# A decoder layer on one core: residual tiles queued behind the second pair of output weights, and two copies of ScalarE at another place

## The reference, cut to what matters

```python
x = _layernorm(x + _L0_attn_ref(x, wq, wk, wv, wo))        # 32 query heads, 8 key/value heads, window of 128
x = _layernorm(x + _L0_xattn_ref(x, ctx, s1, z1, s2, z2))  # matmul of two fake-quantised tensors
x = _layernorm(x + _L0_ffn_ref(x, w_gate, w_up, w_down))   # silu(gate) * up, truncated to int8, down
```

## Time and profile before

| | us |
|---|---|
| median of three runs (1465.59 to 1466.85) | 1465.61 |
| the profiled execution | 1466.88 |
| its span, first to last instruction | 1465.1 |
| TensorE busy | 1429.0 (98%) |
| VectorE busy | 999.4 (68%) |
| ScalarE busy | 782.7 (53%) |
| GpSimd busy | 740.7 (51%) |
| mean granted TensorE clock | 0.996 |

### The profile page before, as it was taken

The page is one execution under the profiler, slowest core; times in us unless marked ns, Lnnn a source line. Parts: engine busy times, 40 slices in busy tenths (PEclk is TensorE's granted clock), DMA queues, the critical chain, the costliest instruction groups (busy, mean ns, idle before and its releaser), DMA issues.

```text
span 1465.1 us, 22782 instructions
## 1 busy us (share of the span) xinstructions
PE 1429.0 (98%) x7024; PEld 1153.3 (79%) x7024; DVE 999.4 (68%) x1768; ACT 782.7 (53%) x1553; POOL 740.7 (51%) x651
## 2 busy tenths in 40 slices
PE   8899999999999999999999999999989999999997
PEld 6688888888888888888888888887657888778643
DVE  7644444445656578888888888887786656566597
ACT  5433333333345466666575666565466555555674
POOL 0477777777565454555455555554476333433100
PEclk9999999999999999999999999999999999999998
DMA  6477877776663757675757676763151222222611
GB/s 230 146 271 283 286 281 270 273 275 256 212 239 108 282 180 277 200 267 179 265 196 271 206 265 209 269 236 127 41 181 74 94 100 81 76 93 86 230 43 74
DMA packets 114330, 283.20 MB, mean 193 GB/s; under 512 B 21216, under 2 KB 21600, under 8 KB 114272
## 3 DMA queue, kind: packets, MB, share of 16 engines
q1 hardware_dynamic: 114272, 282.50, 55.1%
HBM read 184.94 MB, written 95.42 MB: 191 GB/s over the span
## 4 chain that ended last, share of the span: by engine, by line
PE 50%; DVE 7%; ACT 4%; DMA 3%; issue 3%; POOL 2%; SPq 0%; DVEq 0%; ACTq 0%; POOLq 0%
PE ps L1141 7%; PE ps L1143 7%; PE ps L1142 7%; PE ps L1297 6%; PE ps L1298 5%; PE ps L1350 5%; PE ps L1070 2%; PE ps L1071 2%; PE ps L1072 2%; PE ps L1118 2%; PE ps L1117 1%; PE ps L1119 1%; PE ps L1083 1%; DVE u_val L2853 1%; PE ps L1222 1%
## 5 line engine op out<-in xcount | busy, mean ns | idle before, releaser
L1051 PE MATMUL ps<-xo_h,wb_h 128*128 128x512 f32 x644 | 251.6, 391 | 5.2 <-DVE xo_l L2391 2.0
L1053 PE MATMUL ps<-xo_h,wb_l 128*128 128x512 f32 x644 | 250.7, 389 | 0.0
L1052 PE MATMUL ps<-xo_l,wb_h 128*128 128x512 f32 x644 | 250.6, 389 | 0.0
L1141 PE MATMUL ps<-wo_h,o_h 128*128 128x512 f32 x512 | 207.9, 406 | 1.7 <-DMA wo_l<-wo_low 1.7
L1143 PE MATMUL ps<-wo_h,o_l 128*128 128x512 f32 x512 | 200.3, 391 | 0.0
L1142 PE MATMUL ps<-wo_l,o_h 128*128 128x512 f32 x512 | 200.1, 391 | 0.0
L2166 POOL TENSOR_TENSOR pm_l<-pt_l,upto 128x512 fp32r<-128x512 f32 x58 | 74.8, 1290 | 230.4 <-DVE pt_l L2490 230.4
L1517 ACT ACTIVATE wb_h<-wf_l 128x512 fp32r<-128x512 f32 x69 | 43.6, 632 | 197.7 <-DVE wf_l L2419 82.2
L1051 PEld LDWEIGHTS ps<-xo_h,wb_h 128*128 128x128 f32 x644 | 120.9, 188 | 33.2 <-issue 5.8
L1566 ACT ACTIVATE prob<-prob,exp_bias 128x128 f32<-128x128 f32 x256 | 99.8, 391 | 85.6 <-DVE exp_bias L2477 85.6
L2131 POOL TENSOR_TENSOR wb_l<-wf_l,wb_h 128x512 fp32r<-128x512 f32 x66 | 87.8, 1330 | 112.7 <-DVE s_sum L2414 56.8
(11 more groups left out here) (259 smaller groups left out, 3557.8 us busy)
## 6 DMA issues: line engine op xcount, KB each, us to landing
raw<-w_att SPq DMA_DIRECT2D x47, 512.0 KB, 5.4
f_raw<-w_gu SPq DMA_DIRECT2D x44, 512.0 KB, 5.0
u_gu<-f_unit SPq DMA_DIRECT2D x42, 512.0 KB, 4.9
gq<-u_gu SPq DMA_DIRECT2D x42, 512.0 KB, 3.9
wp_raw<-w_att SPq DMA_DIRECT2D x32, 512.0 KB, 5.8
wo_high<-wp_h SPq DMA_DIRECT2D x32, 512.0 KB, 2.8
wo_low<-wp_l SPq DMA_DIRECT2D x32, 512.0 KB, 4.1
q_rows<-c SPq DMA_DIRECT2D x64, 256.0 KB, 2.7
```

Of the source, the lines that this page charges most:

```text
L1051: pe.matmul(prod_ps[i], wh, chunk(xo_h[i], c), start=(i in OPENS and c == 0), stop=False, skip_group_check=True)
L1052: pe.matmul(prod_ps[i], wh, chunk(xo_l[i], c), start=False, stop=False, skip_group_check=True)
L1053: last = pe.matmul(prod_ps[i], wl, chunk(xo_h[i], c), start=False, stop=(c == KH - 1), skip_group_check=True)
L1141: pe.matmul(into, oh, wo_h[half][:, h, :], start=(h == 0), stop=False)
```

## The change

Three pieces of order change; no operation is added or removed.

1. SP: the last four residual tiles of the first group are issued in slot 6 behind the second pair of output weights, and no longer at the end of slot 5.
2. ScalarE: in slots 7 to 9 the whole copy of a turned row stands right behind its rounded copy, and no longer behind `scale_rows`.
3. ScalarE: in slot 10 the copy of bank 6 to `early` stands in front of the second normalisation of row 6, and no longer behind the first two `mixed_high`.

```diff
@@ -825,10 +825,11 @@
                     load_out(g, 0)
                 if j == 6:
                     load_out(g, 1)
-                if first and j in (4, 5):
-                    sp.wait_ge(prod_done, last_product((PS1, PA22)[j - 4]))
-                    for tile in range((j - 4) * TPB, (j - 3) * TPB):
-                        sp.dma_start(resid[:, tile, :], x_rows[tile]).then_inc(x_loaded[j - 4], 16)
+                if first and j in (4, 6):
+                    part = (j - 4) // 2
+                    sp.wait_ge(prod_done, last_product((PS1, PA22)[part]))
+                    for tile in range(part * TPB, (part + 1) * TPB):
+                        sp.dma_start(resid[:, tile, :], x_rows[tile]).then_inc(x_loaded[part], 16)
                 if first and j == 7:
                     for i, source in ((S1, x1_scale), (Z1, x1_zp), (S2, x2_scale), (Z2, x2_zp)):
                         sp.dma_start(param(i), source.rearrange("(a b) -> a b", a=1).to_broadcast([P, 1])).then_inc(prm_loaded, 16)
@@ -1814,6 +1815,7 @@
                 if without_out:
                     if t < TPB:
                         left_high(t)
+                        left_whole(t)
                     elif i < TILES + 5:
                         right_high(t)
                 if i < TILES + 4:
@@ -1827,11 +1829,14 @@
                 if i < TILES + 1:
                     scale_rows(i - 1)
                 if t < TPB:
-                    left_whole(t)
+                    if not without_out:
+                        left_whole(t)
                     if i < TILES:
                         root(0, i)
                     normed(1, i - 4)
                     return
+                if i == TILES + 2:
+                    keep_early(0, 6)
                 if i < TILES + 4:
                     normed(1, i - 4)
                 mixed_high(t, T1L, T1H, 1, 1)
@@ -1842,7 +1847,6 @@
                     keep_early(4, 0)
                     act.activation(ln[:, 0, 21:22], ln[:, 0, 20:21], ACT.Silu)
                 if i == TILES + 2:
-                    keep_early(0, 6)
                     keep_early(1, 7)
                 if i == TILES + 4:
                     keep_early(2, 4)
```

## The result

| | before | changed |
|---|---|---|
| median of seven runs each, same chip | 1466.28 us | 1471.3 us |
| spread | 1465.12 to 1466.85 | 1470.12 to 1472.21 |
| ratio of the changed kernel to the one before | | 1.003, 95% interval 1.0021 to 1.0039 |
| span of the profiled execution | 1465.1 us | 1469.6 us |
| mean granted TensorE clock | 0.996 | 0.994 |

The prediction was 1467.5 us with a range to 1469.2: too low, and the range missed. The loss is 0.3%, clear of the 0.2% that the prediction had set as its mark, so "slower", which had a chance of 0.18.

A forecast was written before the change was run, and what follows sets the result against it. The prediction took TensorE to bound the kernel. Its terms, +2.0 (piece 1), 0 (piece 2) and -0.15 (piece 3), summed to +1.85 on a median of 1465.6: 1467.5 us, range 1463.4 to 1469.2.

The forecast's parts named there:

- The queue catches up: Around 520 us: transfers behind the pause run at mean pace without a straggler; +0.6 - 0.15, 1466.0 us; chance 0.18.
- Both waits of TensorE close: Around 520 us: parameters land ahead of the queue's end, `pt_l` 1.6 us earlier; -1.6 - 0.15, 1463.9 us; chance 0.12.
- The straggler grows: Around 520 us: a late engine hits the longer queue ahead of the parameters again; +3.4 - 0.15, 1468.9 us; chance 0.10.
- Term: +2.0: Around 520 us: parameters land 2.0 us late, moving TensorE's turn of the values from 526.16 to 528.2.
- The clock falls at another place: TensorE's idle stretches move; half clock on the path adds 1.5 us to 1.85, 1469.0 us; chance 0.06.
- Terms of 0 and -0.15: Row slots: moving the whole copies gains 0; the early copy of bank 6 brings the later chain 0.15 us forward.
- The early product counts in full: Row slots: TensorE keeps the 1.8 us of waiting for `early`; with +2.0 that is +0.2, 1465.8 us; chance 0.06.

The follow-up runs named there:

- unfilled waits: Without the 14 needless matmuls one run put where TensorE waits (piece 1, second group of heads written out); that filled run took 1469.34 us, ratio 1.0017.
- the written-out control: The kernel before with piece 1 and TensorE's second group of heads written out instead of looped: 1470.68 us, ratio 1.0025.
- the kernel before with early parameters: The kernel before with the four parameter transfers issued in slot 2 instead of slot 7 of the first group: 1465.95 us, ratio 0.9991.

## Why the prediction was wrong

To add up the terms, single executions must be freed of what differs at the start. I count from the first scores of the attention, near 478 us, where TensorE waits 0.85 us for the same thing (`q_l`) in all of them. In us from there:

| profile | last parameter lands | turn of values | 60 matmuls later | SP issues the last pair of output weights |
|---|---|---|---|---|
| before | 41.5 | 48.1 | 58.6 | 509.3 |
| before, again | 40.6 | 47.3 | 57.7 | 508.0 |
| pieces 2 and 3 | 40.5 | 47.2 | 57.7 | 508.1 |
| piece 3 | 41.4 | 48.1 | 58.5 | 509.2 |
| changed | 42.5 | 49.0 | 61.1 | 511.3 |
| changed, again | 42.8 | 49.7 | 61.9 | 512.4 |
| piece 1 | 42.6 | 49.4 | 61.5 | 511.8 |

Means of the four without piece 1, and of the three with it: the parameters at 41.0 and 42.6 (+1.6), the turn of values at 47.7 and 49.3 (+1.7), 60 matmuls later at 58.1 and 61.5 (+3.4).

1. **Piece 1, the transfers: right, and the size nearly.** The prediction had the parameters and everything behind them 2.0 us late; they are 1.6 and 1.7. That the size fits is in part luck. In the first profile of the change the query load took 4.0 us and not 2.6 (the median of all 64 query loads is 2.7, so the 2.6 was slightly low already). The next query load landed at 511.59 + 7.4 = 518.99, and so the 4.25 MiB behind the first took 11.1 us, the mean pace of the rival "The queue catches up", and not the 12.6 that I had carried over from before. Both errors nearly cancel. By the profiles of the first comparison alone the parameters are only 1.0 us late, by the means 1.6. "The queue catches up" (+0.6), "Both waits of TensorE close" (-1.6) and "The straggler grows" (+3.4) all fall by the means.
2. **Piece 1, the clock: the step that failed.** The prediction says that the 1.2 us won at 517.58 "only makes TensorE arrive earlier and wait longer" and writes "Term: +2.0". The wait was priced as time alone. It grew from 1.0 us to 3.5 to 4.0 in two parts close together, and all four profiles with piece 1 and unfilled waits show half the clock there: 60 matmuls that take 10.5 us took 12.1, 12.1, 12.3 and, in the written-out control, 13.1. That is +1.6 to +2.6 us. I had this mechanism as the rival "The clock falls at another place", with nearly the right price (1.5), but taken from the row slots, not tied to this wait, and with a chance of 0.06. My own forecast said that TensorE would wait "over 3 us" at this place, longer than the 2.3 us behind which the earlier trace rows had already shown the fall; the two in one sum would have been 1.85 + 1.6 = 3.45, or 1469.1.
3. **Pieces 2 and 3: right.** Terms of 0 and -0.15. The context product did wait for VectorE's sum, the first feed-forward product did follow `xb_l` from GpSimd's run, and the turn of row 6 moved by 0.4 at most and the next by nothing; "The early product counts in full" falls. A term of 0.15 is too small for the times to show: the medians of pieces 2 and 3 say +0.4, with an interval from -0.6 to +2.1, and from the first feed-forward product to the turn of row 7 the changed kernel takes 16.17 us instead of 16.19.
4. **What is left.** The medians say +5.0 for the change and +3.9 for piece 1 alone; their intervals (3.1 to 5.7 and 2.5 to 6.0 us) overlap. The table gives +3.4 by 530 us and +3.2 where the last weights are issued (508.6 and 511.8 in the mean). Behind that point one difference counts, at 996 us. (The prediction says that TensorE never idles more than 0.5 us at a time between 530 and 1063 us. In its trace it idled 0.54 there, and in the others more.) TensorE waits 1.5 us in the mean of the three with piece 1 (1.8, 1.3, 1.5) and 1.1 in the four without (0.5, 1.5, 1.2, 1.0), and one of the three has a fall of the clock behind it, +1.5 us there. Spread over the three this is 0.5 + 0.5, so about 1 us in the mean. Whether the change makes it or seven executions are too few to tell stays open. The clock also falls in the row slots, once or twice in each profile without piece 1 and once or not at all in those with it, but there it costs next to nothing: none for the first one, as shown below, and some 0.2 us for the second of the one profile with two (378.2 us from the first feed-forward product to the end, against 377.9 to 378.0 in the other three).

## What to carry to other kernels

A transfer of a few bytes that an engine waits for costs what stands in front of it in the queue: before bulk loads are moved back, look for the small one they now precede, or issue it long before. On the bound engine, a wait that grows must be priced twice, once as time and once as the clock behind it, unless a later wait of that engine takes the slower work up; when two short waits come to stand close together, look in the same trace for the shortest idle stretch behind which the clock fell. A wait taken away within a chain that four engines hand on only changes its name, and the start of the turn after it tells whether anything was won.

## What the runs showed of the hardware

- The half clock came in pieces of 3.4 or 6.8 us. Around 526 us, one of 3.4 us cost 60 matmuls 1.6 us; of two of 6.8 us, one cost 2.6, and one that lay partly over idle time 1.8.
- Equal idle stretches do not always bring it, and it does not always cost. The wait of 2.3 us for `xb_raw` was followed by half clock in both profiles of before, being one. In the kernel before with early parameters it was as long, and the clock stayed up. TensorE's timeline in before, then in that kernel, and the stretch around the first wait there:

```profile
1070.84 1.17 PE L1235 MATMUL ps<-ident,resid 128*128 128x128 f32 x8 [2.29 <-ACT xb_raw L1788]
...
1077.68 1.06 PE L1235 MATMUL ps<-ident,resid 128*128 128x128 f32 x8 [0.52 <-ACT xb_raw L1788]
```

```profile
1068.74 1.06 PE L1235 MATMUL ps<-ident,resid 128*128 128x128 f32 x8 [2.29 <-ACT xb_raw L1788]
...
1075.58 1.06 PE L1235 MATMUL ps<-ident,resid 128*128 128x128 f32 x8 [2.12 <-ACT xb_raw L1788]
```

```profile
1064.00:1072.00 8.00, 5.63 (x37) 2.99 (x37) 7.42 (x27) 6.08 (x9) 7.25 (x6) 1.00 0.42 109
```

  From one turn to the next it is 6.84 us in both. The half clock made the work between them 1.6 us longer, and the wait for ScalarE's next copy became 1.6 us shorter. So what an idle stretch costs in clock is the chance of a fall times the part of it that no later wait takes up: nothing here, 1.6 us or more around 525 us, where the fall came in four of four profiles with piece 1 and unfilled waits.
- Transfers of 128 times 4 bytes took 3.0 to 3.3 us (medians; the last of the four 4.1) directly behind a query load at the end of the weights, and 6.3 to 6.4 (the last 6.65) behind the rest of the weights and 2 MiB of tiles: small ones wait their turn like a large one.
